# Batch 3's rounding gathered between the opening and slot 5 of group 0, the context's late low parts on GpSimd

## The chip, the cores and the metric

One Trainium2 chip, and one of its cores. The metric is the device time of one execution in microseconds (us), as the median of several runs. The five engines of the core are called PE (TensorE, the matrix engine), DVE or VectorE, ACT or ScalarE, POOL or GpSimd, and SP (SyncE, which here only issues DMAs). Each works through its own list of instructions in order; they meet at semaphores, of which every wait in the code names one and a count.

## The reference

A transformer block on `x` of 4 batches x 512 tokens x 512 columns, with a context of the same size:

```python
x = x + xattn(layernorm(x), ctx)          # attention, fp8-rounded linears
x = x + ffn(layernorm(x))                 # 512 -> 1408 -> 512, SiLU gate

def xattn(h, ctx):                        # 8 groups x 2 heads x 128
    h = ln(h, ln_w, ln_b)
    q, k, v = (fp8(h / s) * s @ w.T * w_scale  for q, k, v)      # h-side
    qx      =  fp8(h / s) * s @ wqx.T * w_scale
    kx, vx  = split(ctx @ w_kv_x.T)                              # context, no rounding
    q, k, qx, kx = (ln(each head of 128))
    cat = concat(softmax(q k / sqrt(128)) v, softmax(qx kx / sqrt(128)) vx)
    return fp8(cat / smooth) @ wproj.T * scale

def fp8(y): clip(y, -448, 448) -> bf16 -> float8_e4m3 -> f32
```

Two things matter for the change. First, the projections' input is rounded to fp8, once for each of four scale sets (q, qx, k, v). The kernel does it in bf16 by five VectorE steps: clip; take the exponent bits as a magnitude; bound the magnitude and multiply it; add it to the value; subtract it again. Second, the context is not rounded, so the kernel carries it as two bf16 parts, high (a copy to bf16) and low (context minus high), and both go through PE.

## The kernel before, in words

**Stages.** An opening (0 to 110 us) normalises all four batches of `x`, makes the rounded inputs `xq[b]` (four sets x 4 chunks x 512 tokens), the parts `ctx_hi[b]` and `ctx_lo[b]`, the split weights of group 0, and projects batch 0. Then come 8 groups of 64 slots (`group(g, first, last)`, the same loop over slots on each engine), then the tail: output projection and feed-forward.

**A slot.** Slot s of a group has one unit of attention for each lag: PE multiplies scores of unit s; VectorE takes the row maximum of unit s-1 (line 1429); ScalarE takes two exponentials of it (lines 1032 and 1035, f32 and bf16); GpSimd subtracts them for the low part (`plo`, line 1131); SP transposes by DMA (unit s-3); PE multiplies by v (unit s-5); VectorE scales the result (unit s-6). Beside this PE projects half a tile of the next batch in each slot (line 673), with the sums of squares (line 1321) and the rest of v (line 1327) on VectorE in every second slot, and `head_power` on GpSimd (line 1106). The scores lie in two PSUM banks, so the scores of unit s wait for the exponentials of unit s-2, and these for the maximum.

**Opening, end of VectorE's list.** `quantise(n, b, c, wide)` does the five steps (lines 1257, 1259, 1264, 1268, 1272) for one or two chunks of a batch at once. Lines 1372 to 1376 end the list: roundings of batch 2, then `ctx_rest(1)` (line 1312, the whole low part of context 1), then `quantise(8, 3, 0, 2)`, the first two chunks of batch 3. Group 0 starts behind them.

**Late work in group 0.** The other two chunks of batch 3 are rounded by `quantise_late(c, step)`, one step in each of the slots `LATE_SLOTS` (7 to 30), with the magnitude in `late_mag`, which lies in the place of group 1's weights. The low parts of contexts 2 and 3 are made by `ctx_piece(b, c)` on VectorE, one chunk of 512 columns in each of `CTX_SLOTS` (2 to 30). ScalarE makes the high parts whole (`ctx_part`, line 904); those of contexts 2 and 3 stand between and behind its last parts of the opening (lines 1004 and 1006). `FIRST_PREP` gives the slots in which group 1's weights are made from 6 on.

**Who waits.** PE's batches in group 0 wait for `xq_done` (batch 1 at slot 0, batch 2 at slot 16, batch 3 at slot 32) and for the context parts (slots 9, 25, 41). ScalarE waits before its first exponential for `xq_done` of every opening rounding and for two `ctx_lo_done`, since the attention's buffers lie over the opening's: `p_exp` over `mag`, `pt` over `ctx_raw`, `pp` over `z2`. Contexts 2 and 3 lie in `x_in`, the later place of group 1's weights.

## Time and profile before

| | us |
|---|---|
| median of 3 runs | 1735.4 (1733.77 to 1735.73) |
| the profiled execution | 1738.57 |
| its span, first to last instruction | 1736.7 |

| engine | busy us | share of the span |
|---|---|---|
| PE | 1632.1 | 94% |
| DVE | 1410.2 | 81% |
| ACT | 1359.8 | 78% |
| POOL | 1089.6 | 63% |

The shares are means over stages with different limits. From the page's picture of the span in 40 slices (43.4 us each):

```profile
PE   1569999999999999999999999999999899999999
DVE  8999999999999999999999999998779763323232
PEclk9969999999999999999999999999999999999999
```

A digit is the busy share in tenths; the last line is PE's granted clock in tenths of full. The opening and the start of group 0 are the first five slices. The rows of the section with rows come from windows (busy time of each engine in a stretch, and the granted clock), from timelines (start, duration, engine, line, operation; what stands in brackets is the idle time before it and what ended it), and from the view of one line.

### The profile page before, as it was taken

What the parts mean: (1) busy time and instruction counts of PE and PEld (TensorE: products, weight loads), DVE (VectorE), ACT (ScalarE), POOL (GpSimd) and SP (SyncE); (2) the same over time, 40 slices, a digit from 0 to 9 for tenths busy, and PEclk for the clock granted to TensorE, in tenths of its full rate; (3) what the DMA queues carried; (4) which work ended last, traced back from release to release, by engine and by line L of the source; (5) the groups of instructions that cost most, each with busy time, mean ns of one, the idle gap of its engine ahead of it and who ended that gap; (6) DMA issues with size and microseconds to landing.
All of it is one profiled execution on the core that took longest, in us unless ns stands there. A gap on an engine that the chain in (4) does not pass through costs nothing.

```text
span 1736.7 us, 43799 instructions
## 1 busy us (share of the span) xinstructions
PE 1632.1 (94%) x15491; PEld 1228.0 (71%) x15776; DVE 1410.2 (81%) x3228; ACT 1359.8 (78%) x2908; POOL 1089.6 (63%) x1031
## 2 busy tenths in 40 slices
PE   1569999999999999999999999999999899999999
PEld 1447778888888888888888888888888544444444
DVE  8999999999999999999999999998779763323232
ACT  6978999999999999999999999999999622222221
POOL 1357777777787777777777777778777613121211
PEclk9969999999999999999999999999999999999999
DMA  5947788887888888788878887888999980303000
GB/s 177 223 111 127 140 154 144 148 153 147 148 149 156 147 145 152 147 148 146 151 147 149 148 159 147 145 140 151 188 187 187 196 244 22 138 8 142 4 24 25
DMA packets 663603, 241.45 MB, mean 139 GB/s; under 512 B 619488, under 2 KB 636000, under 8 KB 662880
## 3 DMA queue, kind: packets, MB, share of 16 engines
q1 hardware_dynamic: 662096, 230.20, 68.1%
q0 software_dynamic: 1296, 8.52, 2.4%
q8 instruction: 123, 2.02, 0.5%
q14 instruction: 88, 0.72, 0.1%
HBM read 75.15 MB, written 29.51 MB: 60 GB/s over the span
## 4 chain that ended last, share of the span: by engine, by line
PE 71%; DVE 9%; ACT 7%; issue 5%; POOL 4%; SPq 3%; DMA 2%; DVEq 0%; ACTq 0%; POOLq 0%
PE ps_pj L673 21%; PE ps_s L739 6%; PE ps_o L722 5%; PE ps_o L724 5%; PE ps_o L723 5%; PE ps_s L742 5%; PE ps_s L680 4%; PE ps_qt L692 4%; POOL local L1131 2%; PE ps_s L738 2%; PE ps_pj L811 2%; PE ps_s L825 2%; PE ps_o L811 2%; PE ps_pj L812 2%; PE ps_o L812 2%
## 5 line engine op out<-in xcount | busy, mean ns | idle before, releaser
L1131 POOL TENSOR_TENSOR local<-local 128x512 bf16<-128x512 f32 x512 | 597.1, 1166 | 296.3 <-ACT local L1035 296.0
L673 PE MATMUL ps_pj<-wide 128*128 128x256 bf16 (+1 forms) x5544 | 582.7, 254 | 4.8 <-DVE wide L1214 4.0
L673 PEld LDWEIGHTS ps_pj<-wide 128*128 128x128 bf16 x5544 | 470.1, 98 | 115.0 <-DVE wide L1214 4.4
L1032 ACT ACTIVATE local<-ps_s,neg_max 128x512 f32<-128x512 f32 x512 | 391.8, 765 | 43.7 <-DVE neg_max L1429 41.6
L1035 ACT ACTIVATE local<-ps_s,neg_max 128x512 bf16<-128x512 f32 x512 | 394.0, 770 | 0.0
L722 PE MATMUL ps_o<-v_hi,local 128*128 128x129 bf16 x2048 | 375.5, 221 | 5.7 <-DVE local L1437 3.2
L724 PE MATMUL ps_o<-v_hi,local 128*128 128x129 bf16 x2048 | 375.2, 219 | 0.0
L723 PE MATMUL ps_o<-local 128*128 128x128 bf16 x2048 | 375.1, 218 | 0.0
L1429 DVE TENSOR_REDUCE neg_max<-ps_s 128x1 f32<-128x512 f32 x512 | 344.7, 673 | 22.8 <-PE ps_s L742 22.7
L941 ACT ACTIVATE local<-ps_pj,head_rstd 128x128 f32<-128x128 f32 x756 | 242.0, 448 | 41.8 <-issue 41.7
L1106 POOL TENSOR_TENSOR head_rstd<-sq_sum,minus_half 128x3 f32<-128x3 f32 x256 | 223.4, 873 | 16.4 <-DVE sq_sum L1321 16.4
L1113 POOL TENSOR_TENSOR local<-local 128x512 bf16<-128x512 f32 x192 | 217.8, 1135 | 4.3 <-ACT local L962 4.3
L739 PE MATMUL ps_s<-local 128*128 128x512 bf16 x511 | 194.7, 381 | 17.7 <-ACT local L1035 3.9
L722 PEld LDWEIGHTS ps_o<-v_hi,local 128*128 128x128 bf16 x2048 | 198.7, 97 | 16.7 <-issue 6.8
L723 PEld LDWEIGHTS ps_o<-local 128*128 128x128 bf16 x2048 | 201.6, 98 | 5.5
L724 PEld LDWEIGHTS ps_o<-v_hi,local 128*128 128x128 bf16 x2048 | 197.1, 96 | 0.0
L742 PE MATMUL ps_s<-local 128*128 128x512 bf16 x512 | 195.0, 381 | 0.4 <-POOL local L1113 0.4
L1321 DVE TENSOR_REDUCE sq_sum<-local 128x3 f32<-128x387 f32 x256 | 140.6, 549 | 41.7 <-ACT local L928 38.2
L1437 DVE SCALAR_TENSOR_TENSOR local<-ps_o,r_sum,rsmooth 128x128 bf16<-128x128 f32 x512 | 173.8, 339 | 0.8 <-DVE r_sum L1426 0.5
L1143 POOL TENSOR_TENSOR local<-wide,local 128x512 bf16<-128x512 f32 x44 | 56.8, 1291 | 158.1 <-ACT local L1053 158.1
L928 ACT ACTIVATE local<-ps_pj 128x384 f32<-128x384 f32 x252 | 144.0, 571 | 4.1 <-PE ps_pj L673 0.7
L692 PEld LDWEIGHTS ps_qt<-ident,local 128*128 128x128 f32 x768 | 96.4, 143 | 55.1 <-ACT local L962 15.9
(133 smaller groups left out, 2623.5 us busy)
## 6 DMA issues: line engine op xcount, KB each, us to landing
quantised_heads<-local SPq DMA_DIRECT2D x128, 128.0 KB, 2.4
w_raw<-w_group SPq DMA_DIRECT2D x56, 256.0 KB, 3.2
wide<-quantised_heads SPq DMA_DIRECT2D x3, 4096.0 KB, 13.1
local<-local SPq DMA_TRANSPOSE x640, 3.2
wide<-packed_weights SPq DMA_DIRECT2D x32, 256.0 KB, 3.2
wide<-x SPq DMA_DIRECT2D x6, 1024.0 KB, 12.0
packed_weights<-w_proj POOLq DMA_DIRECT2D x4, 1024.0 KB, 15.2
wide<-quantised_heads SPq DMA_DIRECT2D x16, 256.0 KB, 3.4
```

Source lines behind the costliest of these rows:

```text
L673: last = mm(dst[:, at:at + n], lhs, w_at(par, part, c, cross * 512 + at, n), start=(k == 0), stop=(k == len(terms) - 1))
L722: mm(acc, ph, vh, start=(tc == 0), stop=False)
L723: mm(acc[:, 0:D], ph, vl, start=False, stop=False)
L724: last_mm = mm(acc, pl, vh, start=False, stop=(tc == TT - 1))
L739: mm(ps_s[u % 2][:], q_h, k_l, start=False, stop=False)
L742: mm(ps_s[u % 2][:], q_l, k_h, start=False, stop=True).then_inc(s_done, 1)
L941: last = a(qn[:, i, hs], tile_bank(i, t)[:, hs], ACT.Copy, scale=head_rstd[:, i % 2, h:h + 1])
L1032: a(p_exp[:, u % 2], ps_s[u % 2][:], ACT.Exp, bias=neg_max[:, u % 4:u % 4 + 1])
L1035: a(pp[:, u % PP_BUFS, 0], ps_s[u % 2][:], ACT.Exp, bias=neg_max[:, u % 4:u % 4 + 1])\
L1106: tt_(head_rstd[:, i % 2, 0:3], sq_sum[:, i % 2, 0:3], minus_half[:, 0:3], ALU.pow).then_inc(rstd_done, 1)
L1131: tt_(pp[:, u % PP_BUFS, 1], p_exp[:, u % 2], pp[:, u % PP_BUFS, 0], ALU.subtract)\
L1429: v.tensor_reduce(neg_max[:, u % 4:u % 4 + 1], ps_s[u % 2][:], AX_X, ALU.max, negate=True)\
```

## The change

- `quantise(8, 3, 0, 2)` and `ctx_rest(1)` leave VectorE's opening. All four chunks of batch 3 are now rounded by `quantise_late`, chunk by chunk: 20 steps of 2048 elements. Eight of them stand at the end of the opening, the other twelve in the slots 0, 0, 1, 1, 1, 2, 2, 3, 3, 3, 4, 5. Their magnitude lies in `early_mag`, over `y` and `summed`, which are first written in slot 6.
- The low parts of contexts 1, 2 and 3 move from VectorE to GpSimd, in 12 pieces of 512 columns (`ctx_low`): four between the last `qk_rest` of the opening, four of context 2 in slots 1 to 4 (behind GpSimd's own work of the slot), four of context 3 in slots 8, 14, 20 and 26.
- ScalarE makes context 3's high part not whole in the opening but in four pieces (`ctx_high`) in slots 2 to 5.
- Waits follow: PE and ScalarE count `ctx_piece_done` instead of `ctx_lo_done`, ScalarE's wait at slot 22 for batch 3's rounding goes, and VectorE's `weight_lo` of group 1 waits for the piece of context 3 that lies in its place.

```diff
@@ -194,6 +194,7 @@
         v_lo = carve([2, 2, TT, D], BF16)
         pp = carve([PP_BUFS, 2, T], BF16)
         p_exp = carve([2, T], F32)
+        early_mag = local[:, carve.at:carve.at + SETS * T]
         y = carve([2, T], BF16)
         carve.at += T
         summed = carve([T], BF16)
@@ -248,6 +249,7 @@
         ctx_loaded = sem("ctx_loaded")
         ctx_hi_done = sem("ctx_hi_done")
         ctx_lo_done = sem("ctx_lo_done")
+        ctx_piece_done = sem("ctx_piece_done")
         ln_step = sem("ln_step")
         ln_var = sem("ln_var")
         ln_pow = sem("ln_pow")
@@ -318,14 +320,11 @@
         LN_STEPS = 2 * TT
         ACT_FIRST = 2
         CTX_DIRECT = 2
-        LATE_FROM = 2
-        LATE_SLOTS = (7, 10, 13, 15, 17, 20, 23, 25, 27, 30)
-        CTX_SLOTS = (2, 3, 4, 5, 7, 12, 22, 30)
-
-        late_mag = home(W_FIRST + LATE_FROM * GW)([SETS * T], BF16)
-
-        def ctx_pieces(b):
-            return b + 1 if b < CTX_DIRECT else CTX_DIRECT + CH * (b - CTX_DIRECT + 1)
+        LATE_BEFORE, LATE_SLOTS = 8, (0, 0, 1, 1, 1, 2, 2, 3, 3, 3, 4, 5)
+        CTX_AT = {1: (2, 2), 2: (2, 3), 3: (2, 0), 4: (2, 1), 8: (3, 0), 14: (3, 1), 20: (3, 2), 26: (3, 3)}
+        CTX_HIGH_AT = {2: 0, 3: 1, 4: 2, 5: 3}
+
+
 
         GU_AT = G * HEADS * DM
         WD_AT = GU_AT + CH * 2 * HID
@@ -422,10 +421,10 @@
             return (k // TILES + 1) % 2, k % TILES
 
 
-        OPENING_PIECES = CH + 2 * (B - 1) - 1
+        OPENING_PIECES = CH + 2 * (B - 2)
 
         def pieces_until(b):
-            return CH + 2 * b + (b == B - 1)
+            return CH + 2 * b + (2 if b == B - 1 else 0)
 
         def at_start(t):
 
@@ -762,7 +761,7 @@
                         if first and b + 1 < B and i == 0 and half == 0:
                             pe.wait_ge(xq_done, pieces_until(b + 1))
                         if first and b + 1 < B and i == TT and half == 1:
-                            pe.wait_ge(ctx_lo_done, ctx_pieces(b + 1))
+                            pe.wait_ge(ctx_piece_done, CH * (b + 1))
                         project((b + 1) % B, i, half, (g + 1) % 2 if b == B - 1 else g % 2, GROUP_TILES * g + TILES + k)
 
             for g in range(G):
@@ -902,6 +901,10 @@
             def ctx_part(b):
                 act.wait_ge(ctx_loaded, 16 * (b + 1))
                 a(ctx_hi[b][:], ctx_in(b), ACT.Copy).then_inc(ctx_hi_done, 1)
+
+            def ctx_high(c):
+                act.wait_ge(ctx_loaded, 16 * B)
+                a(ctx_hi[B - 1][:, c], ctx_in(B - 1)[:, c], ACT.Copy).then_inc(ctx_hi_done, 1)
 
             scale_in(0, 0)
             scale_in(0, 1)
@@ -1003,9 +1006,8 @@
             qk_part(-1, 1, 4)
             ctx_part(2)
             qk_part(-1, 2, 5)
-            ctx_part(3)
             act.wait_ge(xq_done, OPENING_PIECES)
-            act.wait_ge(ctx_lo_done, CTX_DIRECT)
+            act.wait_ge(ctx_piece_done, CH)
 
             def group(g, first, last):
                 for slot in slots(last):
@@ -1021,9 +1023,7 @@
                             if n >= 2 * CH:
                                 continue
                             if n == CH and half == 0:
-                                act.wait_ge(ctx_lo_done, ctx_pieces(2))
-                            if n == CH + 2 and half == 0:
-                                act.wait_ge(xq_done, pieces_until(B - 1))
+                                act.wait_ge(ctx_piece_done, CH * 2)
                             weight_hi(n // CH % 2, n % CH, n + 1, half)
                     for u in unit_at(slot, EXP_LAG, first):
                         act.wait_ge(max_done, SLOTS * g + u + 1)
@@ -1034,6 +1034,8 @@
                             act.wait_ge(pt_landed[u % PT_BUFS], 16 * SLOTS // PT_BUFS * g + 16 * (u // PT_BUFS))
                         a(pp[:, u % PP_BUFS, 0], ps_s[u % 2][:], ACT.Exp, bias=neg_max[:, u % 4:u % 4 + 1])\
                             .then_inc(exp_done, 1)
+                    if first and slot in CTX_HIGH_AT:
+                        ctx_high(CTX_HIGH_AT[slot])
                     for k in tile_at(slot, QN_LAG, first, last):
                         head_norm(tile_place(k)[1], GROUP_TILES * g + TILES + k, GROUP_TURNS * g + 3 * (1 + k // TT))
                     for q, j in turn_at(slot, QK_LAG, first, last):
@@ -1113,14 +1115,23 @@
                 tt_(qk_lo[:, b, cross, h], qk_full[:, (q + j) % 2], qk_hi[:, b, cross, h], ALU.subtract)\
                     .then_inc(qklo_done, 1)
 
+            def ctx_low(b, c):
+                pool.wait_ge(ctx_hi_done, b + 1 if b < B - 1 else b + c + 1)
+                tt_(ctx_lo[b][:, c], ctx_in(b)[:, c], ctx_hi[b][:, c], ALU.subtract).then_inc(ctx_piece_done, 1)
+
             for i in range(TILES):
                 head_power(i, i)
                 if i == TILES - 2:
                     qk_rest(-2, 0, 0)
             qk_rest(-2, 1, 1)
+            ctx_low(1, 0)
             qk_rest(-2, 2, 2)
-            for j in range(3):
-                qk_rest(-1, j, 3 + j)
+            ctx_low(1, 1)
+            qk_rest(-1, 0, 3)
+            ctx_low(1, 2)
+            qk_rest(-1, 1, 4)
+            ctx_low(1, 3)
+            qk_rest(-1, 2, 5)
 
             def group(g, first, last):
                 for slot in slots(last):
@@ -1132,6 +1143,8 @@
                             .then_inc(plo_done, 1)
                     for k in tile_at(slot, VAR_LAG, first, last):
                         head_power(tile_place(k)[1], GROUP_TILES * g + TILES + k)
+                    if first and slot in CTX_AT:
+                        ctx_low(*CTX_AT[slot])
 
             for g in range(G):
                 group(g, g == 0, g == G - 1)
@@ -1208,6 +1221,8 @@
                 v.tensor_copy(w_par(par, c * GW, GW), raw(c)).then_inc(w_hi_done, 1)
 
             def weight_lo(par, c, count):
+                if CH < count <= 2 * CH:
+                    dve.wait_ge(ctx_piece_done, CH * 2 + c + 1)
                 dve.wait_ge(w_hi_done, count)
                 hi = w_par(par, c * GW, GW)
                 lo = w_par(par, c * GW + PART, GW)
@@ -1273,16 +1288,15 @@
 
             def quantise_late(c, step):
 
-                n = OPENING_PIECES + c - LATE_FROM
+                n = OPENING_PIECES + c
                 val = xq[B - 1][:, :, c]
-                magnitude = late_mag.rearrange("p (s t) -> p s t", s=SETS)
+                magnitude = early_mag.rearrange("p (s t) -> p s t", s=SETS)
                 dve.wait_ge(quant_step, QUANT_STEPS * n + step)
                 if step == 0:
-                    dve.wait_ge(in_scaled, CH * B)
+                    dve.wait_ge(in_scaled, CH * (B - 1) + c + 1)
                     v.tensor_scalar(val, val, FP8_MAX, -FP8_MAX, ALU.min, ALU.max).then_inc(quant_step, 1)
                 if step == 1:
                     dve.wait_ge(xq_done, n)
-                    dve.wait_ge(ctx_lo_done, ctx_pieces(CTX_DIRECT))
                     dve.sem_inc(waited_dve, 1)
                     v.tensor_scalar(magnitude.bitcast(I16), val.bitcast(I16), EXPONENT, None, ALU.bitwise_and)\
                         .then_inc(quant_step, 1)
@@ -1310,10 +1324,6 @@
             def ctx_rest(b):
                 dve.wait_ge(ctx_hi_done, b + 1)
                 v.tensor_tensor(ctx_lo[b][:], ctx_in(b), ctx_hi[b][:], ALU.subtract).then_inc(ctx_lo_done, 1)
-
-            def ctx_piece(b, c):
-                dve.wait_ge(ctx_hi_done, b + 1)
-                v.tensor_tensor(ctx_lo[b][:, c], ctx_in(b)[:, c], ctx_hi[b][:, c], ALU.subtract).then_inc(ctx_lo_done, 1)
 
             def head_squares(i, t):
 
@@ -1372,8 +1382,8 @@
             quantise(6, 2, 0, 2, {2: (4,), 3: (5,)})
             evacuate(6)
             quantise(7, 2, 2, 2, {3: (7,)})
-            ctx_rest(1)
-            quantise(8, 3, 0, 2)
+            for n in range(LATE_BEFORE):
+                quantise_late(*divmod(n, QUANT_STEPS + 1))
 
             def clip(view):
                 v.tensor_scalar(view, view, FP8_MAX, -FP8_MAX, ALU.min, ALU.max).then_inc(clipped, 1)
@@ -1438,12 +1448,9 @@
                                                r_sum[:, u % 4:u % 4 + 1],
                                                smooth_rows_of(g + H // GROUP_HEADS, H % HEADS), ALU.mult, ALU.mult)\
                             .then_inc(y_done, 1)
-                    for n, at in enumerate(CTX_SLOTS if first else ()):
-                        if slot == at:
-                            ctx_piece(CTX_DIRECT + n // CH, n % CH)
                     for n, at in enumerate(LATE_SLOTS if first else ()):
                         if slot == at:
-                            quantise_late(LATE_FROM + n // (QUANT_STEPS + 1), n % (QUANT_STEPS + 1))
+                            quantise_late(*divmod(LATE_BEFORE + n, QUANT_STEPS + 1))
                     for n in prep_at(g, slot, "sums"):
                         weight_sums(n % CH, n + 1)
                     if last and CLIP_FIRST <= slot < CLIP_FIRST + HEADS_PIECES:
```

## Rows read from the trace of the kernel before

**Rows 1.** Windows: busy us (instructions) of five engines, granted clock, DMA share, GB/s.
```profile
96.10:110.00 13.90, 7.08 (x37) 4.56 (x38) 13.76 (x8) 10.76 (x13) 7.43 (x4) 0.61 0.27 89
110.00:120.70 10.70, 8.61 (x59) 5.71 (x61) 7.84 (x15) 7.92 (x17) 5.64 (x5) 0.68 0.53 64
120.70:160.00 39.30, 36.22 (x382) 28.43 (x387) 38.61 (x88) 32.03 (x73) 28.04 (x26) 1.00 0.63 108
160.00:207.00 47.00, 43.71 (x467) 35.02 (x474) 45.83 (x112) 43.50 (x98) 36.17 (x32) 1.00 0.81 145
275.00:435.00 160.00, 158.31 (x1740) 132.80 (x1771) 151.35 (x367) 152.40 (x341) 125.86 (x122) 1.00 0.82 149
```

**Rows 2.** Timeline of VectorE, the end of the opening and slots 1 and 2.
```profile
96.08 3.17 DVE L1312 TENSOR_TENSOR wide<-local,wide 128x2048 bf16<-128x2048 f32 x1
99.18 2.11 DVE L1257 TENSOR_SCALAR wide<-wide 128x4096 bf16<-128x4096 bf16 x1
...
102.59 2.00 DVE L1264 TENSOR_SCALAR local<-local 128x4096 bf16<-128x4096 bf16 x1
...
106.94 3.06 DVE L1272 TENSOR_TENSOR wide<-wide,local 128x4096 bf16<-128x4096 bf16 x1
109.93 1.27 DVE L1429 TENSOR_REDUCE neg_max<-ps_s 128x1 f32<-128x512 f32 x2
111.13 0.67 DVE L1316 TENSOR_TENSOR wide<-wide 128x512 bf16<-128x512 f32 x1
```

**Rows 3.** Timelines of PE and ScalarE around the first exponentials.
```profile
112.04 0.61 PE L738 MATMUL ps_s<-local 128*128 128x512 bf16 x1 [3.88 <-ACT local L1035]
...
110.72 0.69 ACT L1032 ACTIVATE local<-ps_s,neg_max 128x512 f32<-128x512 f32 x1 [3.86 <-DVE neg_max L1429]
```

**Rows 4.** Timeline of GpSimd at the end of the opening.
```profile
91.54 5.57 POOL L1113 TENSOR_TENSOR local<-local 128x512 bf16<-128x512 f32 x2
97.99 2.22 POOL L1113 TENSOR_TENSOR local<-local 128x512 bf16<-128x512 f32 x1 [0.88 <-ACT local L962]
102.00 1.49 POOL L1113 TENSOR_TENSOR local<-local 128x512 bf16<-128x512 f32 x1 [1.80 <-ACT local L962]
105.14 2.71 POOL L1113 TENSOR_TENSOR local<-local 128x512 bf16<-128x512 f32 x1 [1.65 <-ACT local L962]
```

**Rows 5.** Timeline of VectorE early in the opening: a one-chunk rounding, then context 0.
```profile
26.28 0.69 DVE L1257 TENSOR_SCALAR wide<-wide 128x2048 bf16<-128x2048 bf16 x1
...
30.86 1.22 DVE L1214 TENSOR_TENSOR wide<-w_raw,wide 128x1024 bf16<-128x1024 f32 x1
...
46.45 2.28 DVE L1312 TENSOR_TENSOR wide<-local,wide 128x2048 bf16<-128x2048 f32 x1
```

**Rows 6.** Timeline of VectorE, slots 3 to 6 of group 0.
```profile
114.14 1.32 DVE L1316 TENSOR_TENSOR wide<-wide 128x512 bf16<-128x512 f32 x1
...
118.38 0.56 DVE L1321 TENSOR_REDUCE sq_sum<-local 128x3 f32<-128x387 f32 x1 [0.53 <-ACT local L928]
...
119.05 0.68 DVE L1429 TENSOR_REDUCE neg_max<-ps_s 128x1 f32<-128x512 f32 x1
...
120.25 0.16 DVE L1426 RECIPROCAL r_sum<-ps_o 128x1 f32<-128x1 f32 x1
...
120.71 0.69 DVE L1429 TENSOR_REDUCE neg_max<-ps_s 128x1 f32<-128x512 f32 x1 [0.30 <-PE ps_s L742]
```

**Rows 7.** Timeline of PE in slot 6; timeline of VectorE, maxima of units 35, 36, 47.
```profile
123.18 1.05 PE L673 MATMUL ps_pj<-wide 128*128 128x256 bf16 x8 [0.28 <-ACT local L941]
...
203.42 0.69 DVE L1429 TENSOR_REDUCE neg_max<-ps_s 128x1 f32<-128x512 f32 x1 [0.67 <-PE ps_s L742]
...
206.93 0.67 DVE L1429 TENSOR_REDUCE neg_max<-ps_s 128x1 f32<-128x512 f32 x1
...
235.56 0.67 DVE L1429 TENSOR_REDUCE neg_max<-ps_s 128x1 f32<-128x512 f32 x1
```

**Rows 8.** The view of line 1429: count, minimum/median/maximum ns, first and last start.
```profile
L1429 DVE TENSOR_REDUCE neg_max<-ps_s x512: 659/670/694, 109.9 to 1393.4; 128x1 f32<-128x512 f32 x171
```

## The prediction, made before the changed kernel was run

> **What bounds the kernel now.** I read the table of windows first. Between 275 and 435 us PE is busy 158.3 of 160 us: the steady groups are bound by PE, VectorE follows with 151.4 [rows 1]. The change touches none of that, but only 96 to 203 us. There the table shows three stretches. From 96.1 to 110.0 VectorE is busy 13.76 of 13.90 us, PE 7.1, at a mean granted clock of 0.61. From 110.0 to 120.7 VectorE has 2.9 us idle, with PE at a clock of 0.68 and busy 8.6 of 10.7. From 120.7 to 207 VectorE is busy 84.4 of 86.3 us and PE only 79.9 [rows 1]: VectorE is the bound again, because it rounds batch 3 and makes context parts beside the attention.
>
> The timeline says what the first stretch costs. VectorE runs `ctx_rest(1)` and then the two-chunk rounding, and reaches the first row maximum at 109.93 [rows 2]. ScalarE's first exponential had waited 3.86 us for it, and PE stood 3.88 us until 112.04 for that exponential [rows 3]. What the later stretch costs comes from the maxima. Units 35 to 511 take (1393.4 - 203.4) / 476 = 2.50 us each [rows 7, 8], while from unit 5 (120.71) to unit 35 (203.42) there are 82.7 us for 30 units [rows 6, 7], 7.7 more than 30 x 2.50 = 75.0. So 3.9 + 7.7 = 11.6 us are the most that lies here.
>
> **The unit prices.** A one-chunk rounding with nothing beside it takes 30.86 - 26.28 = 4.58 us for its five steps [rows 5] (about 0.72 for each of the first three, 1.2 for the last two). A maximum takes from 109.93 to 111.13 for two, so 0.60; a pair of squares' sum and rest of v 119.05 - 118.38 = 0.67 [rows 2, 6]. A context low part of one chunk is 0.67 on VectorE [rows 2].
>
> What decides is a price that GpSimd's subtractions put on VectorE. Context 0's `ctx_rest` took 2.28 us with GpSimd idle [rows 5], context 1's the same shape 3.17, with a GpSimd subtraction just before or beside it [rows 2, 4]. In the end of the opening each of GpSimd's subtractions stretches one VectorE step by 0.8 to 0.9: the one that was issued at 97.99 ended at 100.21, and the two-chunk clip of 99.18 took 2.11, where two chunks at 0.69 each [rows 5] would be at most 1.4; that of 102.00 ended at 103.49, and the step of 102.59 took 2.00; that of 105.14 ended only at 107.85, and the last step, of two chunks at 1.2 bare, took 3.06 [rows 2, 4]. The two engines take turns by whole instructions: GpSimd waits for VectorE's step to end, and VectorE's next step waits for GpSimd's. I call this a charge, 0.8 us. A step that reads two tensors of SBUF, or one in bf16 at several elements a cycle, pays it; the maxima, which read PSUM, do not: the maximum of 119.05, of 0.68, ran at its usual length [rows 6, 8]. A context piece of 0.67 that met one took 1.32 [rows 6].
>
> The Trainium skill says the same of the cause (GPSIMD Engine Reference, section 8, Key points: it shares its SBUF interfaces with VectorE, with contention for VectorE instructions in a 2-port mode or with two SBUF inputs); rows 2 and 4 agree and give the price. The rule speaks against this change, since it would make a contender of each of the twelve pieces; taken for every subtraction in slots 1 to 5, which the rows do not bear out, it gives the slower rival's time below.
>
> **Part 1, the end of VectorE's opening.** Removed: from 96.08 to 109.93, 13.85 us, of which four charges are about 3.3, so 10.55 bare. Added before the first maximum: chunks 0 and 1 of batch 3, eight steps in the opening and two in slot 0, 2 x 4.58 = 9.16. GpSimd had four subtractions to run from 96 on; now it has eight, the four pieces of context 1 among them, each 0.95 us behind a VectorE step. VectorE's list there is nothing but steps that pay, so I take eight charges, 6.8: the first maximum falls at 96.1 + 9.2 + 6.8 = 112.1, which is 2.1 us later than before. If the pieces find gaps it is four charges, 3.3, and 108.6. The other end is 112.8, each charge at 0.9 and one more caught. The moved wait on `in_scaled` costs nothing: ScalarE had its whole opening list done at 106.9 (110.72 less 3.86 of idle time [rows 3]), and chunks 2 and 3, scaled before that, are wanted after 112. GpSimd's later `qk_rest` ends by about 108.5; the first cross units that need it come in slot 8. ScalarE's list is shorter by 2 us of `ctx_part(3)`, in a place where it then waited 3.86 us for VectorE [rows 3]: nothing.
>
> **Part 2, slots 1 to 5.** VectorE was busy 7.8 of 10.7 us there [rows 1]. Out go four context pieces. In come chunks 2 and 3. The new bare sum is 5 maxima x 0.60 + 2 x 0.67 + 2 x 4.58 = 13.5 us. Nine GpSimd subtractions fall here, five of exponentials and the four pieces of context 2. An exponential pair is out 2.1 us after its maximum begins (109.93 to 112.04) [rows 2, 3]; placing the nine so, four run wholly or mostly beside maxima and squares, and five meet a rounding step, with 0.3 to 0.9 each, together 3.0. Ends: no charge, 0, and all nine, 7.2. Slot 6 then starts at 112.1 + 13.5 + 3.0 = 128.6, where it started at 120.25 [rows 6]. ScalarE's four high pieces (about 0.5 us each, a quarter of the whole part of 2.0) have cover: it was busy 7.9 of 10.7 us [rows 1] and the slots get longer; without cover they would cost 2. The wait that the cover of `y` and `summed` makes is none, since both are written by VectorE itself, in order, from slot 6.
>
> VectorE is 8.3 us late at slot 6, but PE is not so late, because before it was itself the laggard there (VectorE waited 0.30 for it [rows 6]). PE's tile of slot 6 ran from 123.18 to 124.2 [rows 7]. Now its scores wait for the exponentials of unit 4, whose maximum starts about 126.1: out at 128.2, scores 0.9, tile 1.05, so it ends at 130.1. PE is late by 5.9. Its clock may cost on top: it is at the low level in this stretch already [rows 1] and comes back after a full stretch of work; should it come later, about 1 us.
>
> **Part 3, slots 6 to 35.** Out of VectorE: two roundings, 9.2 bare, and four pieces, 2.4, of 84.4 busy us [rows 1], so it needs 72.8 for the 86.3 us, 2.3 us a slot, and is no bound any more. PE's pace is then 2.50 us, or, where group 1's weights are made as densely as here, (235.56 - 206.93) / 11 = 2.60 [rows 7]; I take 2.55. From the end of PE's tile of slot 6 to the scores of unit 35 are 28.6 slots: 72.9 us (71.5 to 74.4), in place of 203.4 - 124.2 = 79.2. Gain 6.3 (4.8 to 7.7). At 203.42 VectorE waited for PE's scores [rows 7], so both engines stand together and what is won or lost at this point stays to the end. The four pieces of context 3 on GpSimd (busy 64.2 of 86.3 us there [rows 1]) add at most four charges to a VectorE with time to spare. The new waits of `weight_lo` (slots 14 to 46) are for pieces of slots 8 to 26, of ScalarE at slot 12 for one of slot 4: none ends last. No DMA is moved.
>
> **The sum.** Scores of unit 35 at 130.1 + 72.9 = 203.0 against 203.4: 0.4 faster. Against its own time the profiled execution would go from 1738.6 (span 1736.7, 1.9 around it) to 1738.2. It lies 3.2 above the median of the runs; the difference carries over: 1735.4 - 0.4 = 1735.0.
>
> **The rivals.**
> - *No additional charge in the opening.* GpSimd's pieces run where VectorE would have met a subtraction anyway. For it: GpSimd idles 0.9, 1.8 and 1.65 us between its subtractions [rows 4]. Against it: VectorE then has no step that doesn't pay. First maximum at 108.6, all else as forecast: 1735.0 - 3.5 = 1731.5.
> - *The idle time is simply filled.* No charge weighs, the stall of 3.9 goes and the excess of 7.7 too: 1735.4 - 11.6 = 1723.8. Against it: the sum of VectorE's bare steps alone from 96.1 to slot 6 is 9.2 + 13.5, which ends at 118.8, before any charge, so most of the room of 110 to 120 is needed twice.
> - *VectorE becomes the bound in slots 0 to 5 (slower).* All nine subtractions of slots 1 to 5 are charged, 7.2 instead of 3.0, and PE, which stands between units, keeps its low clock into slot 7, 1 us: 1735.0 + 4.2 + 1.0 = 1740.2. It decides from the point where the charges of slots 0 to 5 and the delay of the first maximum pass the 6.3 of part 3, that is where PE's tile of slot 6 ends after 130.5. For it: the margin is 0.4 us. Against it: the maxima give GpSimd its turn once a slot.
> - *The change doesn't relieve slots 6 to 35*, since another limit (ScalarE, 75.5 of 86.3 busy [rows 1]) or the dense weights hold the pace at 2.7: 28.6 x 0.15 = 4.3 of the gain go, 1739.3.
>
> **How the numbers follow.** Forecast 0.50, with own range 1732 to 1738; one rival with fewer charges 0.21 (1731.5); the filled idle time 0.06 (1723.8); the slower one 0.17 (1740.2); no relief 0.06 (1739.3). Range 1729.0 to 1741.0: it takes in all but the filled case and the far ends of the terms. A measurement of this kernel can tell about 0.2%, 3.5 us, from no change, so faster is below 1731.9 and slower above 1738.9. Faster: 0.06, two thirds of 0.21 and 0.05 of the forecast's tail, 0.25. Slower: most of 0.23, and 0.03 of the tail, 0.22. Same: 0.53.
>
> **What would show it.** Part 1: the first maximum at 112 (108.6 for the rival), and opening steps of one chunk in VectorE's timeline at 1.5 to 1.6 us instead of 0.69, one beside each GpSimd subtraction. Part 2: slot 6's first reciprocal at 128.6, rounding steps back to back in slots 1 to 5, PE waiting for exponentials between units. Part 3: maxima from unit 5 to 35 at 2.5 to 2.6 us and VectorE with idle time from 135 us on. Unit 35's maximum at 203.0. Wrong would be a first maximum before 110, or unit 35's maximum more than 4 us from 203.

## The result and the profile after

| | before | after |
|---|---|---|
| median of 12 runs, us | 1734.87 (1733.77 to 1736.34) | 1738.70 (1737.68 to 1739.45) |
| profiled execution, us | 1738.57 | 1738.21 |
| its span, us | 1736.7 | 1736.4 |

The ratio is 1.0021, with a 95% interval of 1.0012 to 1.0030: the change makes the kernel slower, by 3.8 us. The forecast was 1735.0, so 0.4 faster, with a range that held the time; the sign and the size were wrong. The two profiled executions show nothing of the loss, since the one of before ran 3.7 us above its own median. That is a part of the answer, below. That the forecast for the profiled execution, 1738.2, was met to the digit (1738.21) is luck for the same reason.

VectorE at the end of the opening and in slots 0 to 6 (timeline of the changed kernel; it answers to [rows 2, 6]):

```profile
96.04 1.64 DVE L1297 TENSOR_SCALAR wide<-wide 128x2048 bf16<-128x2048 bf16 x1
97.86 1.31 DVE L1301 TENSOR_SCALAR local<-wide 128x2048 int16<-128x2048 int16 x1 [0.19 <-DVE wide L1297]
99.21 1.53 DVE L1304 TENSOR_SCALAR local<-local 128x2048 bf16<-128x2048 bf16 x1
100.77 2.00 DVE L1306 TENSOR_TENSOR wide<-wide,local 128x2048 bf16<-128x2048 bf16 x1
102.80 2.06 DVE L1308 TENSOR_TENSOR wide<-wide,local 128x2048 bf16<-128x2048 bf16 x1
104.78 1.58 DVE L1297 TENSOR_SCALAR wide<-wide 128x2048 bf16<-128x2048 bf16 x1
...
111.86 0.68 DVE L1439 TENSOR_REDUCE neg_max<-ps_s 128x1 f32<-128x512 f32 x1
...
114.06 1.65 DVE L1304 TENSOR_SCALAR local<-local 128x2048 bf16<-128x2048 bf16 x1
115.62 0.68 DVE L1439 TENSOR_REDUCE neg_max<-ps_s 128x1 f32<-128x512 f32 x1
116.22 1.57 DVE L1306 TENSOR_TENSOR wide<-wide,local 128x2048 bf16<-128x2048 bf16 x1
117.82 2.08 DVE L1308 TENSOR_TENSOR wide<-wide,local 128x2048 bf16<-128x2048 bf16 x1
...
127.58 0.68 DVE L1439 TENSOR_REDUCE neg_max<-ps_s 128x1 f32<-128x512 f32 x1
128.17 1.21 DVE L1308 TENSOR_TENSOR wide<-wide,local 128x2048 bf16<-128x2048 bf16 x1
129.31 0.15 DVE L1436 RECIPROCAL r_sum<-ps_o 128x1 f32<-128x1 f32 x1
```

The first five rows are one chunk's rounding. Bare, it takes 4.58 us [rows 5]; here it takes 104.78 - 96.04 = 8.7, since each step lies beside a subtraction of GpSimd. GpSimd's timeline for the same time shows the partner of each: L1115 is `qk_rest`, L1120 a context piece.

```profile
98.58 1.60 POOL L1120 TENSOR_TENSOR wide<-local,wide 128x512 bf16<-128x512 f32 x1
100.14 1.53 POOL L1115 TENSOR_TENSOR local<-local 128x512 bf16<-128x512 f32 x1
101.64 2.13 POOL L1120 TENSOR_TENSOR wide<-local,wide 128x512 bf16<-128x512 f32 x1
103.74 2.06 POOL L1115 TENSOR_TENSOR local<-local 128x512 bf16<-128x512 f32 x1
```

A GpSimd subtraction that lasts 1.1 us alone takes 1.5 to 2.1 in these rows. The ends fit the taking of turns by whole instructions: the piece of 98.58 ends at 100.18, about a bare length behind the end of the VectorE step of 97.86 (99.17), and the VectorE step that was issued at 99.21 ends at 100.74, 0.56 behind the piece, where 0.69 is its bare length. The first maximum is 1.9 us later than before, and slot 6 starts at 129.31 instead of 120.25.

The windows of the changed kernel, for [rows 1]:

```profile
96.10:110.00 13.90, 7.38 (x38) 4.59 (x38) 13.35 (x10) 8.90 (x12) 12.77 (x8) 0.60 0.26 88
110.00:120.70 10.70, 4.88 (x30) 2.68 (x30) 10.41 (x12) 3.59 (x7) 4.12 (x4) 0.68 0.19 37
120.70:160.00 39.30, 35.19 (x344) 26.69 (x345) 35.91 (x80) 33.66 (x76) 31.49 (x28) 0.96 0.52 92
160.00:207.00 47.00, 46.67 (x522) 38.27 (x520) 44.44 (x111) 44.57 (x100) 39.41 (x38) 1.00 0.85 157
```

GpSimd (fifth pair) is busy 12.77 of 13.90 us at the end of the opening, against 7.43 [rows 1]. From 110.0 to 120.7 VectorE works 10.4 us instead of 7.8, and PE only 4.9 instead of 8.6. From 120.7 to 207 VectorE has 5.9 us of idle time, for 1.9 before, and from 160 PE is nearly full.

Rows of PE's timeline show what it stood for in between, its first scores of slot 6 and its tile of that slot; before, there was one wait of over 1 us, of 3.88 [rows 3], and the tile started at 123.18 [rows 7]:

```profile
113.97 0.61 PE L737 MATMUL ps_s<-local 128*128 128x512 bf16 x1 [5.79 <-ACT local L1035]
...
122.61 0.38 PE L737 MATMUL ps_s<-local 128*128 128x512 bf16 x1 [3.25 <-ACT local L1035]
...
129.61 0.39 PE L737 MATMUL ps_s<-local 128*128 128x512 bf16 x1
...
130.90 1.05 PE L672 MATMUL ps_pj<-wide 128*128 128x256 bf16 x8 [0.47 <-ACT local L944]
```

### The profile page after: what moved, and what is told of

It reads as the page before. It is cut to its first block, busy times and chain, and to the rows that moved or that the text cites. A ratio compares the mean times of both kernels' runs of the same rounds, so it can differ in the third digit from the quotient of the medians.

```text
span 1736.4 us, 44101 instructions
## 1 busy us (share of the span) xinstructions
PE 1648.1 (95%) x15776; PEld 1228.7 (71%) x15776; DVE 1412.5 (81%) x3224; ACT 1357.4 (78%) x2911; POOL 1102.5 (63%) x1043
## 4 chain that ended last, share of the span: by engine, by line
PE 83%; DVE 5%; ACT 4%; issue 3%; POOL 2%; DMA 1%; SPq 1%; DVEq 0%; ACTq 0%; POOLq 0%
PE ps_pj L672 26%; PE ps_o L721 6%; PE ps_o L723 6%; PE ps_o L722 6%; PE ps_s L737 6%; PE ps_s L738 6%; PE ps_s L741 6%; PE ps_s L679 4%; PE ps_qt L691 4%; PE ps_pj L810 2%; PE ps_s L825 2%; PE ps_o L810 2%; PE ps_o L811 2%; PE ps_pj L811 2%; PE ps_s L824 2%
## 5 line engine op out<-in xcount | busy, mean ns | idle before, releaser
L944 ACT ACTIVATE local<-ps_pj,head_rstd 128x128 f32<-128x128 f32 x756 | 241.0, 445 | 39.6 <-issue 39.5
L1115 POOL TENSOR_TENSOR local<-local 128x512 bf16<-128x512 f32 x192 | 213.4, 1111 | 0.0
L737 PE MATMUL ps_s<-local 128*128 128x512 bf16 x512 | 194.9, 381 | 12.6 <-ACT local L1035 11.4
L741 PE MATMUL ps_s<-local 128*128 128x512 bf16 x512 | 194.8, 380 | 0.8 <-POOL local L1115 0.8
L738 PE MATMUL ps_s<-local 128*128 128x512 bf16 x512 | 195.0, 381 | 0.0
```

Source lines behind the costliest of these rows:

```text
L737: mm(ps_s[u % 2][:], q_h, k_h, start=True, stop=False)
L738: mm(ps_s[u % 2][:], q_h, k_l, start=False, stop=False)
L741: mm(ps_s[u % 2][:], q_l, k_h, start=False, stop=True).then_inc(s_done, 1)
L944: last = a(qn[:, i, hs], tile_bank(i, t)[:, hs], ACT.Copy, scale=head_rstd[:, i % 2, h:h + 1])
```

## Experiments

All times were compared with the kernel before on the same chip; three chips were used (rounding alone, pieces alone, high part whole and steps spread on one; changed again, the two with tiny pieces and the one with pieces one slot ahead on the second; the second profile of before and the mended kernel on the third). The start of each unit's row maximum on VectorE is the clock by which I compare them: unit 0 is the first maximum, unit 5 stands in slot 6, at unit 35 PE and VectorE stand together again. The second profiles of the two kernels keep their distance from there (3.43 us at unit 35, 3.46 at unit 498); the first profile of before loses more on its way, as the last section of the experiments shows.

| kernel | unit 0 | unit 5 | unit 35 | median us (before beside it) | ratio, 95% interval |
|---|---|---|---|---|---|
| before | 109.93 | 120.71 | 203.42 | 1734.87 | |
| before, second profile | 109.40 | 120.15 | 202.13 | 1735.45 (1735.32) | 1.0003 (0.9993 to 1.0013) |
| changed | 111.86 | 129.38 | 206.12 | 1738.70 (1734.87) | 1.0021 (1.0012 to 1.0030) |
| changed, again | 111.28 | 128.80 | 205.56 | 1738.97 (1735.68) | 1.0018 (1.0009 to 1.0027) |
| first pieces tiny | 109.50 | 127.04 | 203.85 | 1737.31 (1735.68) | 1.0007 (0.9997 to 1.0016) |
| all pieces tiny | 109.44 | 124.84 | 201.55 | 1734.09 (1735.68) | 0.9991 (0.9982 to 1.0000) |
| rounding alone | 110.42 | 129.08 | 205.44 | 1739.11 (1735.42) | 1.0021 (1.0012 to 1.0030) |
| pieces alone | 109.29 | 120.30 | 202.48 | 1734.89 (1735.42) | 0.9996 (0.9987 to 1.0005) |
| high part whole | 111.16 | 128.69 | 205.23 | 1738.11 (1735.42) | 1.0014 (1.0004 to 1.0023) |
| steps spread | 105.06 | 118.14 | 201.70 | 1734.02 (1735.42) | 0.9992 (0.9983 to 1.0001) |
| spread, pieces one slot ahead | 105.15 | 118.00 | 205.22 | 1743.29 (1735.68) | 1.0041 (1.0027 to 1.0055) |
| spread, mended | 105.22 | 118.05 | 200.57 | 1733.53 (1735.32) | 0.9989 (0.9980 to 0.9998) |

### Do GpSimd's pieces hold VectorE?

```diff
+            for b in range(1, B):
+                nc.gpsimd.memset(ctx_lo[b][:].rearrange("p c t -> p (c t)"), 0.0)
...
             def ctx_low(b, c):
                 pool.wait_ge(ctx_hi_done, b + 1 if b < B - 1 else b + c + 1)
-                tt_(ctx_lo[b][:, c], ctx_in(b)[:, c], ctx_hi[b][:, c], ALU.subtract).then_inc(ctx_piece_done, 1)
+                n = 4 if b == 1 else T
+                tt_(ctx_lo[b][:, c, 0:n], ctx_in(b)[:, c, 0:n], ctx_hi[b][:, c, 0:n], ALU.subtract).then_inc(ctx_piece_done, 1)
```

This is the kernel with the four pieces of context 1 at 4 of their 512 columns; in the other, `n = 4` stands for all twelve. Both leave out most of the low part. Beside them ran the changed kernel once more.

> The changed kernel unchanged, as the neighbour of the next three on the same chip. Every theory: 1738 to 1739.5 us, first maximum at 111.9, slot 6 at 129.3, unit 35 at 206.1.

> The changed kernel, but GpSimd's four pieces of context 1 compute 4 of their 512 columns (the rest of that low part is zero, so the output misses it); their places, waits and signals stay. Theory of charges (a piece of 512 columns beside a rounding step costs VectorE about 0.75 us): the first maximum comes 2.6 to 3.2 us earlier than in the changed kernel, at 108.7 to 109.3, slot 6 at 126.1 to 126.8, unit 35 at 203 to 203.8, time 1735.3 to 1736.3. Rival (the stretched rounding steps are their own semaphores and waits, not GpSimd): the first maximum within 0.5 us of 111.9, time 1738 to 1739.5.

> The same with all twelve pieces at 4 columns (the low parts of contexts 1 to 3 are left at zero). Theory of charges: besides the 3 us of the opening, slots 1 to 5 lose the three charges that pieces of context 2 make there (0.35, 0.7 and 0.35 in the changed kernel) and the queue ahead of the power: slot 6 at 124 to 125.5, unit 35 at 200.5 to 202.5, time 1733 to 1735. Rival (slots 1 to 5 are bound by the count of rounding steps alone): slot 6 exactly as much earlier as the first maximum, unit 35 as in the last one.

VectorE's list in the opening with all pieces tiny (its timeline):

```profile
96.78 0.68 DVE L1300 TENSOR_SCALAR wide<-wide 128x2048 bf16<-128x2048 bf16 x1
97.65 1.31 DVE L1304 TENSOR_SCALAR local<-wide 128x2048 int16<-128x2048 int16 x1 [0.19 <-DVE wide L1300]
98.99 1.62 DVE L1307 TENSOR_SCALAR local<-local 128x2048 bf16<-128x2048 bf16 x1
100.64 1.23 DVE L1309 TENSOR_TENSOR wide<-wide,local 128x2048 bf16<-128x2048 bf16 x1
101.91 1.22 DVE L1311 TENSOR_TENSOR wide<-wide,local 128x2048 bf16<-128x2048 bf16 x1
103.05 1.58 DVE L1300 TENSOR_SCALAR wide<-wide 128x2048 bf16<-128x2048 bf16 x1
...
106.27 2.00 DVE L1309 TENSOR_TENSOR wide<-wide,local 128x2048 bf16<-128x2048 bf16 x1
...
109.44 0.68 DVE L1442 TENSOR_REDUCE neg_max<-ps_s 128x1 f32<-128x512 f32 x1
```

From the first rounding step to the first maximum there are 12.66 us, in the changed kernel 15.82: 3.16 less for four pieces, 0.79 each. Of the ten steps ahead of the maximum only four are still stretched, by 0.6 to 0.9 (1.31, 1.62, 1.58 and 2.00), one beside each of the four `qk_rest` of this stretch, where it was eight; the first, with only a tiny piece beside it, has its bare length (0.68). The rival, that the steps' own semaphores stretch them, falls.

The first maximum comes only 1.8 us earlier than in the neighbour, since with the added clearing (5.28 us at the head of GpSimd's list) everything behind it is 1.3 later: GpSimd's first power starts at 10.46 instead of 9.12, and the first rounding step at 96.78 instead of 95.46. So the first kernel missed what I expected, by at most 0.2 us at the first maximum, at slot 6 and at unit 35, and by 1 us in the time. The second was inside it. (The neighbour itself, the changed kernel again, stood 0.6 us earlier than its first trace at all three marks, as its first rounding step did already, 95.46 for 96.04.)

With the eight other pieces tiny too, slots 1 to 5 shorten by another 2.1 us (unit 0 to unit 5: 15.40 against 17.54), and the gain holds at unit 35 (2.3) and in the time (3.2). I had expected it, from charges and from the piece in GpSimd's queue ahead of the power; the two shares were not told apart. The rival, that only the count of rounding steps matters there, falls too. But even this kernel, rid of the work of all twelve pieces on either engine, is only 1.6 us under before (ratio 0.9991, 0.9982 to 1.0000), or about 3 if the 1.3 of the clearing are given back to it, which is an estimate.

### Each part alone

The rounding moved, all low parts on VectorE. ScalarE's four high pieces in slots 2 to 5 stay as in the changed kernel:

```diff
+        CTX_SLOTS = (2, 3, 4, 5, 7, 12, 22, 30)
...
-            ctx_low(1, 0)
...
-                    if first and slot in CTX_AT:
-                        ctx_low(*CTX_AT[slot])
...
+            ctx_rest(1)
             for n in range(LATE_BEFORE):
                 quantise_late(*divmod(n, QUANT_STEPS + 1))
...
+                    for n, at in enumerate(CTX_SLOTS if first else ()):
+                        if slot == at:
+                            ctx_piece(CTX_DIRECT + n // CH, n % CH)
```

> The changed kernel with the rounding moved, but every low part back on VectorE as before: the whole of context 1 ahead of batch 3's steps, eight pieces in slots 2 to 30. Theory of charges (each GpSimd subtraction beside a VectorE step that reads SBUF through both ways costs it 0.8 us): the pieces of context 1 cost VectorE on GpSimd (four charges, 3.3) a bit more than on VectorE (2.3), so the first maximum comes at 111.0 (111.9 changed kernel) and slot 6 at 129 (129.3), unit 35's maximum at 205 to 207; time 1737.5 to 1739.5, the loss of the change stays. Rival (GpSimd's subtractions cost VectorE nothing, the chunks were only too long): the first maximum 2.3 later than in the changed kernel, slot 6 at 134, time 1742 or more.

Unit 0 at 110.42, 0.6 earlier than expected, unit 5 at 129.08, 1739.1 us: the whole loss of the change is there with the low parts back on VectorE. So a context piece costs VectorE about the same on either engine in this place: 0.67 of its own work, or a charge of 0.79. Against the changed kernel's first trace, VectorE's end of the opening is 0.7 us shorter (15.12 for 15.82) and slots 1 to 5 are 1.1 longer (18.66 for 17.52).

The kernel before with only the eight pieces of contexts 2 and 3 on GpSimd:

```diff
-        CTX_SLOTS = (2, 3, 4, 5, 7, 12, 22, 30)
+        CTX_AT = {1: (2, 2), 2: (2, 3), 3: (2, 0), 4: (2, 1), 8: (3, 0), 14: (3, 1), 20: (3, 2), 26: (3, 3)}
...
+                    if first and slot in CTX_AT:
+                        ctx_low(*CTX_AT[slot])
...
-                    for n, at in enumerate(CTX_SLOTS if first else ()):
-                        if slot == at:
-                            ctx_piece(CTX_DIRECT + n // CH, n % CH)
```

> The kernel before with one part of the change alone: the eight low pieces of contexts 2 and 3 on GpSimd (slots 1 to 4, 8, 14, 20, 26), the rounding as before. Theory (VectorE bounds slots 6 to 35 of the kernel before, and pieces that meet maxima cost it little): first maximum stays at 109.9, slot 6 within 1 us of 120.2, since PE at its low clock and the stall set it, unit 35's maximum 2 to 4 us earlier than 203.4; time 1731 to 1733. Rival (the charge eats what leaves VectorE, 0.67 against 0.8 a piece): unit 35 within 1 us of 203.4, time 1734.5 to 1736.

Unit 35 at 202.48, where the second profile of before has 202.13, and 1734.9 us: no measurable difference. My theory's 2 to 4 us didn't come. The rival fits: from 120.7 to 203.4 VectorE is busy 80.74 us, as it was before (80.94), so the charges eat what leaves it. GpSimd's timeline shows also a second way in which a piece costs, its place in a list that is worked in order:

```profile
143.54 3.42 POOL L1135 TENSOR_TENSOR local<-local 128x512 bf16<-128x512 f32 x2
146.92 1.83 POOL L1106 TENSOR_TENSOR head_rstd<-sq_sum,minus_half 128x3 f32<-128x3 f32 x1
148.72 1.15 POOL L1118 TENSOR_TENSOR wide<-wide 128x512 bf16<-128x512 f32 x1
149.83 1.09 POOL L1113 TENSOR_TENSOR local<-local 128x512 bf16<-128x512 f32 x1
```

The piece (L1118) has the `qk_rest` (L1113) behind it, for which PE's scores wait. By the view of waits PE stood 1.8 us for L1113, once, between 120 and 203 us; in the kernel before it was 0.4 us, twice.

### The high pieces on ScalarE

```diff
             qk_part(-1, 2, 5)
+            ctx_part(3)
...
-                    if first and slot in CTX_HIGH_AT:
-                        ctx_high(CTX_HIGH_AT[slot])
```

> The changed kernel with context 3's high part made whole in the opening, as before, and no high pieces in slots 2 to 5. Theory (ScalarE's piece of 0.5 us and the power behind it stand ahead of the head norm for which PE's tile of slot 6 waits): that tile ends at 131.4 instead of 131.95, unit 35 about 0.5 us earlier, time 1738.0 to 1738.7. Rival (the pieces on ScalarE are the missing 3 us of the forecast): unit 35 at 203 to 204 and time 1735 to 1736.

PE's tile of slot 6 started at 129.69 without a wait; in the second trace of the changed kernel it started at 130.32 after one of 0.47 for the head norm. Of these 0.6 us, 0.1 is an earlier maximum of unit 4. Unit 35 came 0.33 earlier than in that trace and 0.89 than in the first, and the time was 0.6 to 0.9 lower, on another chip than the second trace, with ratios whose intervals overlap (1.0004 to 1.0023 against 1.0009 to 1.0027), so the time alone does not show a gain. The rows do: a high piece of about 0.5 us was on PE's path. In ScalarE's timeline of the changed kernel's second trace the exponentials end, then comes the piece (L907), and only then the head norm (L944) for which PE waits.

```profile
128.29 0.68 ACT L1035 ACTIVATE local<-ps_s,neg_max 128x512 bf16<-128x512 f32 x1
128.86 0.63 ACT L907 ACTIVATE wide<-wide 128x512 bf16<-128x512 f32 x1
129.38 0.88 ACT L944 ACTIVATE local<-ps_pj,head_rstd 128x128 f32<-128x128 f32 x3
```

The rival, that all that was missing lies here, falls: unit 35 at 205.23, not at 203 to 204.

### A smaller step in the same direction

One chunk ahead of group 0, the second by one step in each of the slots 1 to 5, chunks three and four in slots 7 to 30 as before; the eight pieces on GpSimd.

```diff
-            quantise(8, 3, 0, 2)
+            quantise(8, 3, 0, 1)
-        LATE_SLOTS = (7, 10, 13, ...)
+        LATE_SLOTS = (1, 2, 3, 4, 5, 7, 10, 13, ...)
```

> As the last one, and only one chunk of batch 3 is rounded ahead of group 0, the second by one step in each of the slots 1 to 5, the third and fourth as before in slots 7 to 30. Theory (the stall ahead of the first exponential is VectorE's opening list, and what fills slots 0 to 5 must stay under about 2.9 us): first maximum at 106 (109.9 before), PE's stall of 3.9 us gone or under 1 us, slot 6 at 116 to 118, unit 35 at 196 to 199; time 1727 to 1731. Rival (room ahead of slot 6 doesn't matter, since VectorE has to do the same steps by slot 35 in any case): unit 35 as in the last one, time within 1 us of it.

The first maximum came at 105.06, 0.9 earlier than expected, and PE's wait for its exponential shrank to 0.71. But of the 4.3 us gained at unit 0 (against the second profile of before) 2.0 are left at unit 5 and 0.4 at unit 35; the time is 1734.0, within 1 us of the pieces alone, where I had hoped for 1727 to 1731. The rival had this right: VectorE is busy 80.8 of the 82.7 us from 120.7 to 203.4, and what it hasn't done before it must do there. Between units 0 and 5, where 2.3 us went, its timelines show VectorE standing still for most of that:

```profile
111.52 1.83 POOL L1107 TENSOR_TENSOR head_rstd<-sq_sum,minus_half 128x3 f32<-128x3 f32 x1
...
113.44 0.94 ACT L942 ACTIVATE local<-ps_pj,head_rstd 128x128 f32<-128x128 f32 x3 [2.72 <-issue]
...
114.43 1.09 PE L674 MATMUL ps_pj<-wide 128*128 128x256 bf16 x8 [2.66 <-ACT local L942]
...
114.79 0.56 DVE L1331 TENSOR_REDUCE sq_sum<-local 128x3 f32<-128x387 f32 x1 [2.15 <-ACT local L929]
```

GpSimd took up the power only at 111.5, behind a context piece and an exponentials' subtraction, and it lasted 1.83 us instead of 0.85, with a VectorE step of two SBUF inputs beside it until 112.6; the head norm, PE's tile and VectorE followed in a chain. Behind that stand PE's granted clock fell as well: 0.83 from 114 to 116, 0.50 from 116 to 118.

So the next kernel kept context 2's pieces on VectorE in slots 2 to 5, and put context 3's on GpSimd in slots without a power.

```diff
+        CTX_SLOTS = (2, 3, 4, 5)                                        # VectorE
+        CTX_AT = {13: (3, 0), 23: (3, 1), 35: (3, 2), 40: (3, 3)}       # GpSimd
```

> The kernel with the rounding steps spread, and its context pieces placed where they cost least by what the runs so far show: context 2's four pieces on VectorE in slots 2 to 5 (it sat idle 2.2 us there, waiting behind a power that GpSimd ran late), context 3's four on GpSimd in slots 13, 23, 35, 40, none in a slot with a power. Theory (GpSimd's power behind pieces held PE's tile of slot 4 for 2.7 us): no idle time over 1 us in slots 3 to 5, slot 6 at 117 to 118, unit 35 at 199.5 to 201, time 1731.5 to 1733.5. Rival (VectorE's sum of work alone counts): unit 35 at 202 to 203, time 1734 to 1735.5.

This was a mistake of mine, and of use. Up to unit 13 it stood at 138.43, 2.3 us ahead of the kernel above. Then VectorE's weight step of slot 14 waited 2.4 us for a piece that GpSimd makes in slot 13, since VectorE came to it before GpSimd had made the piece, and the late step held the maxima behind it. The same came back at two more pieces. The view of waits:

```profile
DVE wide L1224 <- POOL wide L1120: 7.4, 3, 2.5
```

7.4 us in three waits; 1743.3 us, 7.6 slower than before. Mended with the pieces in slots 9, 19, 27 and 35:

> The spread kernel with context 2's pieces on VectorE, and context 3's pieces on GpSimd in slots 9, 19, 27 and 35, each at least five slots ahead of the weight step that waits for it (the last try had them one slot ahead, and VectorE waited 7.4 us for GpSimd, which works a slot behind it). Theory: up to unit 13 as the last try (138.4), no wait of VectorE for a piece, unit 35 at 199 to 200.5, time 1731 to 1733. Rival (VectorE's sum of work by slot 35 alone counts): unit 35 at 201.7 to 203, as with the spread steps alone, time 1734 to 1735.5.

Unit 13 at 138.47, no such wait, unit 35 at 200.57, just outside what I expected, and 1733.5 us, above the 1731 to 1733 that I expected: 1.8 us under before, ratio 0.9989 (0.9980 to 0.9998), the best of the kernels here. Its windows show VectorE without a gap and PE at full clock from 110.0 to 120.7, where the kernel with spread steps left VectorE idle for 2.5 us at a mean clock of 0.84:

```profile
110.00:120.70 10.70, 9.21 (x98) 6.52 (x97) 10.67 (x22) 7.64 (x18) 7.13 (x7) 1.00 0.64 106
120.70:160.00 39.30, 37.10 (x386) 28.70 (x384) 38.81 (x90) 33.62 (x75) 30.76 (x27) 1.00 0.67 117
```

The theory (power) and the rival (sum of work) both hold in part: of the 2.3 us that it is ahead of the kernel with spread steps at unit 13, 1.1 survive to unit 35. In the time the two are 0.5 us apart, on different chips, which is within their scatter.

### Which profile of before?

> The kernel before unchanged, for a second profiled execution. Theory (the profiled execution of before lost over a microsecond in groups 3 to 7 and some more in the tail by chance, its time being 3.2 above its median): the same maxima as before up to unit 64 within 0.7 us, and an end 2 to 4 us earlier than 1736.7. Rival (its profile always costs 3 us): end at 1736 to 1737.

The second profiled execution of the same kernel ends at 1732.6, not at 1736.7. At unit 0 the two differ by 0.5, from unit 6 to 290 by 1.2 to 1.3, at unit 498 by 2.6, at the end by 4.1. The 0.8 that come in slots 1 to 5 have a place: PE's granted clock. Windows of PE, first profile:

```profile
110.00:112.00 2.00, 0.00 (x0) 0.61 0.00 0
112.00:114.00 2.00, 1.96 (x7) 0.50 0.00 0
114.00:116.00 2.00, 2.00 (x9) 0.50 0.68 131
116.00:118.00 2.00, 1.95 (x19) 0.68 0.71 135
```

and the second:

```profile
110.00:112.00 2.00, 0.49 (x3) 1.00 0.00 0
112.00:114.00 2.00, 2.00 (x11) 0.58 0.00 0
114.00:116.00 2.00, 2.00 (x15) 0.56 0.68 131
116.00:118.00 2.00, 2.00 (x23) 1.00 0.74 143
```

In the first the clock fell to the 1.2 GHz level while PE stood for the first exponential, and PE was at it from its first scores on (112.04, of 0.61 us). In the second PE stood as well, but its first scores, at 111.51, still ran at 2.4 GHz (0.39 us); the clock fell only behind them, in the window from 112, and was back at 116. By the share of the two levels in each window, an estimate, the fall came 1.9 us later than in the first profile and the return 1.5 us earlier. What made the rest of the distance, after unit 290, I did not look into.

## Why the prediction was wrong

The price that it built on, GpSimd's charge on VectorE, was right, and the first maximum with it. What failed is the path to PE's tile of slot 6, which came 1.9 us later than forecast, and with smaller errors in the pace and in the baseline this turned a balance of two large terms, called at -0.4 us, into a loss of 3.8.

- **The unit prices** stood. The charge of 0.8 a subtraction was measured directly, 0.79. (The prediction says that context 0's low part ran "with GpSimd idle"; rows 5 do not show GpSimd. Its timeline has only the issuing of DMAs there.)
- **Part 1** stood: first maximum 112.1 forecast, 111.86 and 111.28 in the two traces, eight steps stretched. Its upper end, 112.8, does not follow from its words: nine charges at 0.9 would give 113.4.
- **Part 2, the charges of slots 1 to 5**, was 1.1 us too small. The walk gave five charges, 3.0 us. The trace has six stretched steps, 1.65, 1.57, 2.08, 1.37, 1.53 and 1.57, where 0.69, 1.21, 1.22, 0.69, 0.69 and 1.21 are bare: 4.1 us. Slot 6 started at 129.31 for 128.6.
- **PE's tile of slot 6** was the step that failed most. The prediction started unit 4's maximum at 126.1, let the exponentials and the scores follow, and the tile follow the scores directly, to end at 130.1. The tile began at 130.90 and ended at 131.95. Most of these 1.9 us come from VectorE: unit 4's maximum started at 127.58, 1.5 late, since all six stretched steps stand ahead of it and the last rounding step, behind it, ran bare (128.17, 1.21). The scores so started at 129.61 for 128.2. The other 0.47 is PE's wait for a head norm that stands on ScalarE behind a high piece. I had written of those pieces "have cover", by ScalarE's busy share; one of them had none (high part whole).
- **Part 3, the pace**: from the tile's end to unit 35 there were 206.12 - 131.95 = 74.2 us, for 72.9 at the value I took, inside its bounds. The relief itself came: from unit 5 to 35 it is 76.7 us, for 82.7. But it isn't the context pieces' doing, to which part 3 gives 2.4 of its 11.6 us. The rounding alone does it in 76.4 us with four pieces still on VectorE, and the pieces alone bring nothing.
- **The baseline.** The tile and the pace give unit 35 at 206.1 for 203.0: 3.1 us, a loss of 2.7 against before where 0.4 of gain was forecast. The times differ by 3.8, so 1.1 are left for "the difference carries over". The span of before from which I subtracted had run long, and I had seen it 3.2 above the median; part of that excess lay inside the stretch that I compared, where the second profile of before is 1.3 earlier (203.42 and 202.13). Against that profile the change loses 4.0 us at unit 35, and 3.4 by its own second trace. (Against 1735.0 the measured time is only 3.7 over, since the median of before is 1734.87 from all runs, not 1735.4.)

Of the rivals, the one that the change doesn't relieve slots 6 to 35 came nearest in its number, 1739.3, but by luck: it takes 4.3 us from the gain by a pace of 2.7 us, and the trace has 74.2 / 28.6 = 2.59. The slower one, 1740.2, is 1.5 over, and its mechanism is in the trace in part: charges in slots 1 to 5, but 4.1 us and not 7.2, and a low clock, but not into slot 7. PE's clock fell twice. It was at 0.64 from 110 to 112, as PE stood, and at 0.50 from 112 to 116; it fell again behind PE's stand of 3.25 us (1.00 from 122 to 124, 0.55 from 124 to 126) and was back at 1.00 from 128 on, before slot 6. What this second fall cost was not measured by itself; VectorE, without a wait for PE from 111.86 to 129.38, was late there in any case. The filled idle time (1723.8) and the case without further charges (1731.5) fall with the first maximum, at 111.86 and not at 108.6 or before, and with the tiny pieces.

## What to carry to other kernels

Idle time of an engine is room only for work that doesn't contend with its neighbour and that fits before the next wait: here the 10.8 us of slots 1 to 5 had 2.9 idle, and 9.2 us of rounding were put in for four pieces of 0.67 taken out. Moving an elementwise piece from VectorE to GpSimd saved nothing here, since it then held VectorE's SBUF steps for about as long (0.79 us) as it had taken itself (0.67), and it delayed what stood behind it in GpSimd's ordered list. Where a forecast is the small difference of two terms, take the baseline from more than one profile, and when work of one engine is to be ready for another, look at when each engine comes to it: two lists are not at the same slot number at the same time. And to say when an engine goes on, follow every instruction that it waits for to its place in the other engine's list; a busy share does not tell that a short piece has cover.

## What was not expected of the hardware

Two profiled executions of the same kernel differed by 4.1 us in their span (1736.7 and 1732.6), while its timed runs spread over 2.6 us (1733.77 to 1736.34); PE's clock fell 1.9 us later in the second and came back 1.5 us earlier (the estimates above), and a part of the distance arose there. Durations repeat (the low part of context 1 took 3.17 us in both), positions do not: 0.5 us apart at unit 0, 1.3 at unit 35, 4.1 at the end. A difference of a few us between two kernels is not to be read from one profile of each.
